# A fused attention and mixture-of-experts layer: roots on ScalarE, earlier loads, later routing, and unread products on TensorE

## What is computed

```python
xn = layernorm(x)
p = einsum('bsd,ed->bse', xn, Wv) + bv       # q = k = v = p, 16 heads of 8
attn = softmax(p_heads @ p_heads^T / sqrt(8))
s = (attn @ p_heads) @ Wo^T + bo
z = layernorm(xn) * ln_g + ln_b
probs = softmax(z @ rW + rb)                 # 8 experts, the best 2, weights w
hid = gelu(z @ W1[e] + b1[e])                # 256 wide
mixed = sum over the 2 of w * (hid @ W2[e] + b2[e])
out = x + s * silu(xn + mixed)
```

## Time and profile before

| what | value |
|---|---|
| median of three runs | 629.43 us (628.19 to 631.27) |
| the profiled execution | 632.46 us, span of its instructions 630.7 us |
| granted clock of TensorE, mean | 0.936 |
| TensorE, ScalarE, VectorE busy | 571.2, 543.2, 240.1 us |
| chain that ended last | TensorE 74%, ScalarE 9%, VectorE 7%, issue 5%, DMA 4% |
| a step with no use of the bank, steady | 1.81 us |
| a step with an `up` or a `down`, steady | 2.07 us |
| one split on GpSimd, start to start | 2.9 us |
| ScalarE's table load and what follows it, from 268.63 | 1.30 us |
| 32 scatters of half 0, 84.61 to 127.6 | 43.0 us |
| first exponential of step 0, of step 255 | 52.7 us, 620.5 us |

### The profile page before, as it was taken

The page is one execution under the profiler, slowest core; times in us unless marked ns, Lnnn a source line. Parts: engine busy times, 40 slices in busy tenths (PEclk is TensorE's granted clock), DMA queues, the critical chain, the costliest instruction groups (busy, mean ns, idle before and its releaser), DMA issues.

```text
span 630.7 us, 11527 instructions
## 1 busy us (share of the span) xinstructions
PE 571.2 (91%) x3990; PEld 232.3 (37%) x3990; DVE 240.1 (38%) x695; ACT 543.2 (86%) x591; POOL 230.1 (36%) x252
## 2 busy tenths in 40 slices
PE   3778884799999999799999999999988999999996
PEld 2553320223344344333444344434334343433221
DVE  5553863573333333113222232223232852223381
ACT  4576663699999999979999999999999999999994
POOL 2364047827777774254211121112203334341000
PEclk9977776799999999869999999999995999999999
DMA  6137697746466655227363445453233654442220
GB/s 164 45 101 219 231 304 276 184 132 149 110 162 133 162 96 116 70 67 160 68 153 99 127 112 132 103 135 108 70 117 108 173 167 139 130 116 83 65 66 19
DMA packets 100989, 81.54 MB, mean 129 GB/s; under 512 B 54219, under 2 KB 92638, under 8 KB 100318
## 3 DMA queue, kind: packets, MB, share of 16 engines
q1 hardware_dynamic: 94270, 71.26, 43.2%
q0 software_dynamic: 6656, 9.48, 4.8%
HBM read 58.07 MB, written 28.39 MB: 137 GB/s over the span
## 4 chain that ended last, share of the span: by engine, by line
PE 74%; ACT 9%; DVE 7%; issue 5%; DMA 4%; SPq 1%; ACTq 0%; DVEq 0%
PE bank_v L1330 35%; PE pair L1276 16%; PE bank_f L1370 8%; PE bank_f L1379 8%; ACT exps L776 7%; DMA p_dram<-w_ring 3%; PE bank_f L1347 2%; PE pair L1236 1%; ACT pre L752 1%; PE bank_f L1343 1%; PE pair L1227 1%; DMA x_tok<-in_L_attn_x 1%; DVE o_turned L1082 1%; PE bank_f L1354 1%; DVE v_tok L863 1%
## 5 line engine op out<-in xcount | busy, mean ns | idle before, releaser
L776 ACT ACTIVATE exps<-pair 128x1024 f32<-128x1024 f32 x512 | 488.9, 1049 | 54.6 <-PE pair L1276 36.3
L1330 PE MATMUL bank_v<-exps,v_tok 128*32 128x512 f32 x2048 | 285.0, 630 | 3.1 <-ACT exps L776 1.6
L687 POOL DMA_INDIRECT o_dram<-o_ring,slot_place x80 | 77.4, 968 | 238.3 <-DVE o_ring L1133 238.0
L1276 PE MATMUL pair<-q_ring,k_ring 26*128 26x512 f32 x1024 | 152.9, 513 | 2.7 <-ACT exps L776 2.1
L1276 PEld LDWEIGHTS pair<-q_ring,k_ring 26*128 26x128 f32 x1024 | 60.7, 188 | 93.4 <-ACT exps L776 54.8
L672 POOL DMA_INDIRECT z_dram<-pre,dest_i x64 | 64.3, 1004 | 52.2 <-DVE place_i L1037 33.3
L1379 PEld LDWEIGHTS bank_f<-w_ring,pre 128*128 128x128 f32 x320 | 46.2, 208 | 72.2 <-issue 43.3
L1124 DVE TENSOR_TENSOR pre<-bank_f,w_ring 128x256 f32<-128x256 f32 x80 | 33.9, 423 | 102.1 <-PE bank_f L1370 102.1
L1379 PE MATMUL bank_f<-w_ring,pre 128*128 128x128 f32 x320 | 62.5, 322 | 9.7 <-ACT pre L752 5.3
L1133 DVE TENSOR_TENSOR o_ring<-bank_f,w_ring 128x128 f32<-128x128 f32 x80 | 23.2, 290 | 124.3 <-PE bank_f L1379 121.1
L679 POOL DMA_INDIRECT place_dram<-token_place,place_i x64 | 61.3, 958 | 19.5 <-issue 19.5
(11 more groups left out here) (154 smaller groups left out, 287.1 us busy)
## 6 DMA issues: line engine op xcount, KB each, us to landing
w_ring<-w_dram SPq DMA_DIRECT2D x80, 192.0 KB
w_ring<-w_dram SPq DMA_DIRECT2D x80, 129.0 KB
q_ring<-p_dram SPq DMA_DIRECT2D x56, 104.0 KB
k_ring<-p_dram SPq DMA_DIRECT2D x56, 96.0 KB
z_dram<-s_tok SPq DMA_DIRECT2D x4, 1280.0 KB, 13.1
z_ring<-z_dram SPq DMA_DIRECT2D x80, 64.0 KB
rows_in_sb<-o_dram SPq DMA_DIRECT2D x16, 256.0 KB, 2.9
p_dram<-z_ring SPq DMA_DIRECT2D x8, 256.0 KB, 2.9
```

Source lines behind the costliest of these rows:

```text
L687: pool.indirect_dma_start(o_dram[:, :], bass.IndirectOffsetOnAxis(slot_place[:, h, 4 * k + i:4 * k + i + 1].bitcast(U32), 0), o_ring[:, q ...
L776: nc.scalar.activation(exps[:, g % ES, 2 * half:2 * half + 2, :], pair[(2 * g + half) % 3][:, :, :], ACT.Exp, scale=SCALE).then_inc(exp_do ...
L1276: ins = nc.tensor.matmul(pair[h % 3][:, j % 2, :], k_ring[32 * j:32 * j + KROWS, n % 2, kt * P:(kt + 1) * P], q_ring[32 * j:32 * j + KROWS ...
L1330: ins = nc.tensor.matmul(bank_v[32 * j:32 * j + 32, :], v_tok[:, (n // HG) * KT + kt, first:first + 32], exps[:, g % ES, j, :], start=(kt ...
```

## The change

- Roots. ScalarE takes the square root (its first table is that of the root now), VectorE a reciprocal and one Newton round (`invert`). Norm 2 takes its root in the prologue and the rest (`norm2`) after all blocks, ahead of `keep_router_bias`. Statistics are no longer put between the links of a chain. After the last block ScalarE loads the table of the exponential.
- Loads. x chunk 2 is loaded ahead of the small rows. The high part of blocks 0 and 1 is stored three times, so unit 0 takes 8 loads; the copy within `p_dram` covers only blocks 2 to 7. Unit 1, rb, W1, bo and the zeros of z_dram0 are issued after the stores of block 7, W1, rb and bo no longer after block 3.
- Later routing. Half 0's ranks move from steps 2 to 5 to 6 to 8, and what follows them by 3 or 4 steps; the norms from 13 to 18 to 27, 28, 30, 31, 33 and 34; bias is four uses of four columns in 22, 23, 25, 26 instead of eight of two; W1's scaling to 27 to 30; the second scatter from 31 to 36, and with it `keep_w2` and `clear_places` to g = 38; MOE_AT from 37 to 41, so `load_z(0)` to g = 38, the first `up` to 41, the gelus to 92 and 188, the last `down` to 232, the last combining to 250. `load_w1(0)` and `(1)` are at g = 35 and 37.
- Unread products. The four behind the branch go. 12 whole-array products (128x128 by 128x128) go ahead of the first scores, which now all come after the rows of block 7; two ahead of each half of scores in steps 1 to 4; 24 ahead of the first half of the step after each gelu step.

```diff
-KQ_FIRST = PART_LOADS + 4
+EXACT_LAST = PART_LOADS + 2 * 4
...
-WARM = (4, 4)
+WARM = 4
+WARM_GAP = 12
+WARM_STEP = 2
+WARM_GELU = 24
+WARM_AT = range(1, 5)
...
-RANK_AT = ((2, 3, 3, 4, 4, 5), (17, 18, 19, 20, 22, 23))
-COUNT_AT = (7, 24)
-ASSIGN_AT = ((7, 8, 8, 9, 10), (25, 26, 27, 28, 30))
-SCALE_Z_AT = ((5, 6, 7, 8), (18, 20, 22, 23))
-EXP_AT = (10, 21)
-WEIGH_AT = ((12, 13, 14), (31, 32, 33))
-BIAS_AT = 4
-BIAS_COLS = 2
-NORM_AT = 12
-ZERO_AT = 12
-SCALE_W1_AT = (13, 14, 15, 16)
-SCATTER_AT = (11, 31)
-MOE_AT = 37
+RANK_AT = ((6, 6, 7, 7, 8, 8), (17, 18, 19, 20, 22, 23))
+COUNT_AT = (11, 24)
+ASSIGN_AT = ((11, 12, 12, 13, 14), (25, 26, 27, 28, 30))
+SCALE_Z_AT = ((9, 10, 10, 11), (18, 20, 22, 23))
+EXP_AT = (14, 21)
+WEIGH_AT = ((15, 15, 16), (31, 32, 33))
+BIAS_AT = 22
+COPY_HI_AT = 14
+BIAS_COLS = 4
+NORM_AT = 27
+ZERO_AT = 8
+SCALE_W1_AT = (27, 28, 29, 30)
+SCATTER_AT = (15, 36)
+MOE_AT = 41
...
-PLACE_AT = (54, 77)
+PLACE_AT = (59, 82)
...
-        place(("norm", g), NORM_AT + g - EARLY)
+        place(("norm", g), NORM_AT + (g - EARLY) * 3 // 2)
...
             load_x(1)
+            load_x(2)
...
-                for part in range(PARTS):
-                    row = (HI_ROW, LO_ROW)[part]
-                    sp.dma_start(p_dram[:, row:row + DK, tokens], (p_hi, p_lo)[part][:, g % 2, :]).then_inc(parts_stored[g % 2], 16)
+                hi_rows = (0, HI_ROW, LO_ROW + DK) if g < EARLY else (HI_ROW,)
+                for row in hi_rows:
+                    sp.dma_start(p_dram[:, row:row + DK, tokens], p_hi[:, g % 2, :]).then_inc(parts_stored[g % 2], 16)
+                sp.dma_start(p_dram[:, LO_ROW:LO_ROW + DK, tokens], p_lo[:, g % 2, :]).then_inc(parts_stored[g % 2], 16)
...
+                    load_keys(0)
                     sp.wait_ge(m_kept[0], 16 * EARLY)
                     sp.wait_ge(m_zeroed, 32)
-                    sp.wait_ge(ring_cleared, 1)
-                    for j in range(4):
-                        load_head(0, 0, j, 0, kq_in[0])
-                        load_stabiliser(0, j, kq_in[0])
-                if g == 3:
-                    sp.dma_start(w1_stage, W1.rearrange("e h f -> h e f")).then_inc(w1_staged, 16)
...
+                    load_queries(0)
+            load_unit(1)
+            sp.dma_start(rb_bc[:, :], rb.rearrange("(a d) -> a d", a=1).broadcast_to([P, E])).then_inc(bias_in, 16)
+            sp.dma_start(w1_stage, W1.rearrange("e h f -> h e f")).then_inc(w1_staged, 16)
+            sp.dma_start(bo_bc[:, :], bo.rearrange("(a d) -> a d", a=1).broadcast_to([P, D])).then_inc(bias_in, 16)
+            zero_z(0)
...
-                if g == 2:
+                if g == COPY_HI_AT:
                     for row in (0, LO_ROW + DK):
-                        sp.dma_start(p_dram[:, row:row + DK, :], p_dram[:, HI_ROW:HI_ROW + DK, :]).then_inc(hi_copied, 16)
+                        sp.dma_start(p_dram[:, row:row + DK, EARLY * BLK:], p_dram[:, HI_ROW:HI_ROW + DK, EARLY * BLK:]).then_inc(hi_copied, 16)
...
-                    if g == (AT["up", q - 2, 3] + 1 if q >= 2 else MOE_AT - 8 + 2 * q):
+                    if g == (AT["up", q - 2, 3] + 1 if q >= 2 else MOE_AT - 6 + 2 * q):
                         load_w1(q)
...
+            root(0)
             normalise(0)
             for s in range(NB + 1):
                 if s + 1 < NB:
                     normalise(s + 1)
+                if s == 0:
+                    root(1)
                 if s < NB:
                     copy_xT(s)
+                if 1 <= s < 3:
+                    root(s + 1)
                 if s >= 1:
                     project(s - 1)
+            act.wait_ge(act_dummy_ready, 1)
+            nc.scalar.activation(act_dummy[:, :], ident[0:1, 0:1], ACT.Exp).then_inc(act_dummy_ready, 1)
...
+            def invert(root, variance):
...
+                link(nc.vector.reciprocal(root, root))
+                link(nc.vector.scalar_tensor_tensor(out=some, in0=root, scalar=-0.5, in1=root, op0=ALU.mult, op1=ALU.mult))
+                link(nc.vector.tensor_tensor(some, some, variance, ALU.mult))
+                link(nc.vector.scalar_tensor_tensor(out=root, in0=some, scalar=1.5, in1=root, op0=ALU.add, op1=ALU.mult))
...
+            take(8)
             sum_gram()
-            norm1(0, *NORMS[0], lambda: beside_norm(0))
+            norm1(0, *NORMS[0], keep_m2)
             router_weights()
-            norm1(1, *NORMS[1], statistics)
-            assert statistics() is None
-            keep_p(0)
+            take(8)
+            norm1(1, *NORMS[1])
+            take(16)
             norm1(2, *NORMS[2])
-            for g in range(1, NB):
+            variance2()
+            for g in range(NB):
                 keep_p(g)
...
-                elif g == 4:
-                    norm2()
...
+            norm2()
             keep_router_bias()
...
+                if g in WARM_AT:
+                    keep_warm(WARM_STEP, pair[h % 3][:, 0, 0:P])
+                if g - 1 in GELU_AT and half == 0:
+                    keep_warm(WARM_GELU, pair[h % 3][:, 0, 0:P])
...
-                keep_warm(WARM[1])
                 prologue()
-                first_scores(0)
                 rows_p(NB - 1)
-                first_scores(1)
-                first_scores(2)
+                pe.wait_ge(n2_copied, EARLY)
+                keep_warm(WARM_GAP, spare_v)
+                for h in range(3):
+                    first_scores(h)
```

More of the change, by code:

```diff
@@ L41 @@
 PARTS = 2
+EARLY_PARTS = 4
 PROWS = 3 * DK
@@ L47 @@
 SCALE = float(DK) ** -0.5
-RSQRT_SEED = 0x5F3759DF
-NEWTON = 3
 N2_LIMIT = 400.0
@@ L388, in build, with stored @@
         out_rows = out.rearrange("b s d -> (b s) d")
+        def stored(g):
+            return 16 * (EARLY_PARTS + g // 2 * PARTS)
         def written(*use):
@@ L410, in _ @@
             sp.dma_start(rw_sb[:, :], rW).then_inc(small_in, 16)
-            for c in range(2, len(X_CHUNKS)):
+            for c in range(3, len(X_CHUNKS)):
                 load_x(c)
@@ L442, in load_stabiliser, with load_keys, load_queries, load_unit @@
                              p_dram[(n % HG) * 4 + j, M_ROW:HEAD_ROWS, tokens]).then_inc(loaded, 16)
+            def load_keys(n):
+                for j in range(4):
+                    sp.dma_start(k_ring[32 * j:32 * j + PROWS, n % 2, :].bitcast(F32),
+                                 p_dram[(n % HG) * 4 + j, 0:PROWS, (n // HG) * S:(n // HG + 1) * S]).then_inc(kq_in[n % 2], 16)
+            def load_queries(n):
+                for j in range(4):
+                    sp.dma_start(q_ring[32 * j:32 * j + KROWS, n % 2, :].bitcast(F32),
+                                 p_dram[(n % HG) * 4 + j, HI_ROW:HEAD_ROWS, (n // HG) * S:(n // HG + 1) * S]).then_inc(kq_in[n % 2], 16)
+            def load_unit(n):
+                if n >= 2:
+                    sp.wait_ge(pv_done, (n - 1) * US)
+                if n == HG:
+                    sp.wait_ge(hi_copied, 32)
+                    for i in range(2):
+                        sp.wait_ge(m_kept[1 + i], (NB - EARLY) // 2 * 16)
+                load_keys(n)
+                load_queries(n)
             for g in range(NB):
@@ L479, in _ @@
             with sp.If(m2_bits > M2_LIMIT_BITS):
-                sp.wait_ge(kq_in[0], 16 * KQ_FIRST)
+                for i in range(2):
+                    sp.wait_ge(kq_in[i], 16 * KQ_LOADS)
                 with sp.Fori(0, NU // 2) as w:
@@ L717, in _, with root @@
             bv_col = cols[:, E * FC + 2:E * FC + 3]
+            def root(c):
+                act.wait_ge(variance_ready, c + 1)
+                if c < len(NORMS):
+                    some = slice(NORMS[c][0], NORMS[c][0] + NORMS[c][1])
+                    nc.scalar.activation(rstd[:, some], veps[:, some], ACT.Sqrt).then_inc(root_ready, 1)
+                else:
+                    nc.scalar.activation(rstd2[:, :], veps2, ACT.Sqrt).then_inc(root_ready, 1)
             def normalise(g):
@@ L887, in keep_logits, with take @@
                 dve.wait_ge(logits_kept, h + 1)
-            def beside_norm(c):
-                if c == 0 and links[0] == 7:
-                    keep_m2()
-                else:
-                    statistics()
-            for t in range(7):
-                statistics()
-            link(statistics())
+            def take(count):
+                for _ in range(count):
+                    ins = statistics()
+                link(ins)
+            take(8)
             sum_gram()
-            norm1(0, *NORMS[0], lambda: beside_norm(0))
+            norm1(0, *NORMS[0], keep_m2)
             router_weights()
-            norm1(1, *NORMS[1], statistics)
-            assert statistics() is None
-            keep_p(0)
+            take(8)
+            norm1(1, *NORMS[1])
+            take(16)
             norm1(2, *NORMS[2])
-            for g in range(1, NB):
+            variance2()
+            for g in range(NB):
                 keep_p(g)
```

80 lines of the change are left out of this document (29 added, 51 removed).

## The result

The changed kernel takes 651.8 us (median of 4 runs, 650.7 to 657.7), the kernel before, run beside it, 630.1 (628.2 to 631.3): 1.037 times the time, 95% interval 1.030 to 1.043 (by the medians alone 1.034; one of the four runs took 657.7). It is slower, by 22 us; forecast were 628 us and a range of 604 to 641. The profiled execution took 651.7 us with a span of 650.0, 19.3 more than before, so its rows speak for the median.

What follows compares the result with a forecast made beforehand. Bound by ScalarE's two exponentials a step where they run back to back, with time lost in the head to waits for scores. -12.0 + 1.0 + 2.0 + 7.4 = -1.6 gave 630.9 us profiled, median 628; range 604 to 641.

Steps and rivals of the forecast that it cites:

- (c): Steps 19 to 34: the 12.8 us wait for norm stores goes; step 34 starts at 120.8 us, against 145.7.
- (b): Steps 10 to 19: VectorE waits for bo, landing at 61.2 us; turn_out starts at 69.4, step 19 at 88.1.
- (d): Step 42: z waits in SP's queue behind W2's copy, TensorE stands 13 us; start 150.0 against 162.0, 12.0 gained.
- (a): Prologue and first steps: first exponential at about 43.6 us, 9 earlier; products add 2.8 in steps 1 to 4, covered.
- its gap of about 5: Head: a sign that the forecast is right, a gap of about 5 us before step 11, ended by L1082.
- Rival A: Step 42: no hole, as SP gets z there early; it starts at 135.5 us, kernel 611.5; chance 0.17.
- the 10 to 15 that were to be the sign of it: Step 42: a sign that the forecast is right, a gap of 10 to 15 us ended by the transpose of z.
- The pauses: Behind both gelus: the 24 products delay the fourth step by 2.6 and 4.8 us, +7.4 in sum.
- Rival B: Pauses: the products buy the clock back at once, or it never falls; -0.4 instead of 7.4, kernel 620 us; chance 0.20.
- Rival C: Pauses: the 24 products run at half rate throughout, 11.4 us per burst; +16 instead of +7.4, 636.6 us; chance 0.18.
- 1.0 and 2.0 forecast: Behind step 42: 1.0 us for four bank uses now after it, 2.0 for half clock behind the hole.
- the upper end of the range: Whole kernel: 641 us, which is the 24 products at half rate throughout with 3 us on top for bo.

Runs made afterwards that it cites:

- e12: The changed kernel without the 12 products ahead of step 0 and the two in each of steps 1 to 4: 652.2 us.
- e5: The changed kernel with the store of scaled W1 issued at step 33 instead of 31: 651.3 us.
- e3: The changed kernel with W2's copy, b2's loads and the clearing of places issued at step 20 instead of 38: 642.4 us.
- e1: The changed kernel without the 24 products behind the burst in each gelu pause: 640.9 us.
- e6: The changed kernel with five edits: no pause products, rb and bo early, W2's copy at step 20, rows' loads first, W1's store at step 33: 612.0 us.
- e11: e8 with 8 products ahead of each burst's first down and one ahead of each other down, none behind: 607.6 us.
- e4: The changed kernel with the combined rows' loads ahead of unit and W2 loads, and those from tile 12 on one step earlier: 646.7 us.
- e8: e6 also without the products ahead of step 0 and in steps 1 to 4: 607.8 us.
- e7: The kernel before, with only 24 products added in the first score step behind each gelu: 641.1 us.
- e9: e8 with W1's store back at step 31: 611.5 us.

## Why the prediction was wrong, point by point

The profiled execution was forecast at 630.9 us and took 651.7. Of the 21 us, 15.5 lie ahead of T(42) and 5.4 behind it. Two steps of the forecast failed outright: (c), that nothing would hold the norms' stores, and the sentence that nothing else changes behind step 42. Two terms, bo in (b) and SP's queue in (d), were the right mechanism at too small a size.

- **(a) The prologue and the first steps: right.** T(0) 44.8 for 43.6; m2 is there at 11.3 for 9.9; steps 1 to 4 take 3.1 over 1.81 each for 2.8 (in e12, without products, 1.3, so the products' own part is less), and e12 shows the claim that they cost nothing there: they were covered. The twelve take 2.84 for 2.7.
- **(b) "bo lands 5.6 after its issue at 55.6": mis-sized.** The mechanism is what happened, VectorE in keep_router_bias, ranks and turn_out behind it. But SP's queue was 3.0 later (58.64), as the last split's stores ended at 54.2 for 51.1, and the landing 1.3 longer, so turn_out came at 73.6 for 69.4. T(11) came at 77.2, where the forecast's T(10) of 64.5, a step and its gap of about 5 give some 71.2: 6.0 us. So 3.0 are the walk over the splits, 1.3 the landing, and the rest lies between turn_out and step 11, where TensorE was at half clock (66.9 to 80.5), which no term of this walk has. The last steps to T(19) took 18.3 for 16.9.
- **(c) "The wait for norm stores (12.8 in rows 2) goes": wrong.** Of the 12.8 us, 3.5 are left. The zeros were no longer in its way, but W1's scaling and its store were, which the change moves to the same steps. I counted both groups of stores as moved and didn't put them in one queue. Step 34 took 6.3 us instead of 1.8. e5 shows the cause, and that it alone decides nothing.
- **(d) SP at step 38: mechanism right, size short by 7.3 us** (T(34) to T(42) 36.5 for 29.2). The loads of W1 took 8.25 for 8.3, but started 8.9 after T(34) for 4.0, as SP stood for the norms that (c) had let go. W2 and b2 took 10.8, where I had 8.7 and kept the rows' 10.2 as a bound. e3 shows that the place of the copy is worth 9.4 us. ScalarE stood 15.9 us ahead of step 42, just over the 10 to 15 that were to be the sign of it. Rival A, no hole, had 0.17 and is out.
- **The pauses: right**, +3.5 and +4.1 for +2.6 and +4.8. The 24 products took 7.28 us for 7.1. Against the kernel before, that is; e1 gives back 10.9, since its own tails are 8.2 and 8.8. Why they are shorter than the 10.7 and 9.4 before is open: e6, whose instructions there are the same as e1's, has 10.8 and 8.7, so part of the 10.9 may be e1's luck with the clock. Rival B, products that pay, is out: where they do keep the clock (e11), they are ahead of the burst. Rival C asked for 11.4 us behind each burst and didn't come.
- **"Outside these, nothing in the change touches the 214 steps from 42 on but the count of bank uses": wrong.** Between steps 42 and 88 the bank uses and the half clock together cost 1.3 (1.0 and 2.0 forecast), but the later start of the experts shifted the rows' loads against unit 13's, which keeps its step: a load that came ahead of it before is now behind it. The 18 steps from the fourth behind the second pause on took 43.8 us instead of 37.5: 6.3 us. e4 shows it: the idle time ahead of step 199 goes from 5.23 to 0.19 us.
- **The sign.** Each of the four terms missed was a loss, and the upper end of the range took only two of them, at 3 us for bo and 1.5 for W2. A change that re-times everything on an in-order queue has more places to lose than to win; the rivals should have held one more, that two moved items meet in SP's queue.

By the runs, then: the parts that were meant to speed the head do so (e8 stands 23 us below the kernel before, with them all in), and 44 us were given away: 10.9 by the products in the pauses, 9.3 by bo's place, 9.4 by W2's and 5.1 by the rows', one by one, 4.2 by the head's products once nothing hides them, and the other 5.1 by W1's store and by how the places act on each other, which the runs don't part. The Trainium skill, page "TensorE: Matmul & The Clock Gate", Part 1: The HAM clock gate, has it that activity releases the throttle; e11 agrees (0.70 to 1.00). e1 and e7 show what such products cost where they stand ahead of real work.

## What to carry to other kernels

When a step of a schedule moves, list everything that its queue issues between the old and the new place, and everything that moves there too; a transfer that nobody awaits soon (W2's copy) belongs in a stretch where the queue stands idle, and a small one that an engine stands for (bo, two tiles of rows) goes ahead of bulk. Test the places one by one: an edit that gains nothing alone (e5) may be worth it when the hole behind it is closed (e9, not clear of noise), and products that cost nothing today (e12) cost 4 us once the wait above them is gone. Work that only keeps a clock up must lie where the engine is idle, and even there it gained nothing measurable here (e11); between the last awaited product and the next scores, 7.3 us of it cost 2.4 to 6.0 us a pause (e7, e1).

## What was not expected of the hardware

- The clock's return behind a pause varies between kernels whose instructions there are the same: 4.7 us after the first gelu in e1, 10.6 in e6, so the four steps behind it took 8.2 and 10.8 us. One profile of each was kept, so whether it also varies between executions of one kernel isn't known. A difference of 2 us between two such kernels shouldn't be put down to what was edited.
- With 13 products in the gaps of a burst TensorE was granted the full clock (1.00) over the 15.5 us of the first pause, and without them 0.70.
- The issue of b2's eight broadcast loads took 8.48 us at step 20 as well (7.78 at step 38, 7.56 before), so it was dear in all three places. In each, the first of the eight took 3.1 to 4.0 us and the others 0.6.
